# A decoder layer on one core: the last softmax sums on GpSimd, the gates spread by unit 14, two experts ahead of the shared one

## The chip, the cores and the metric

The kernel runs on one core of one Trainium2 chip. The metric is the time of one execution in microseconds on the device; the kernel before took 257.47 us (median of 3 runs, 257.4 to 257.64). TensorE, VectorE, ScalarE, GpSimd and the SyncE queue each run their own list of instructions in program order and meet only at semaphores.

## What is computed

One decoder layer over 2 batches of 256 tokens of width 256, normed after each block: self-attention with latent projections, cross-attention to 512 context rows with latent keys, and a mixture of 8 experts (2 picked per token) with one shared expert. The last stage is the one that matters here:

```python
def _moe(x, gate, expert_bias, w1, w2, w3, shared_w1, shared_w2, shared_w3):
    scores = sigmoid(xt @ gate.T)
    _, sel = top_k(scores + expert_bias, 2)
    ...
    for e in range(NUM_EXPERTS):
        h = silu(xb @ w1e.T) * (xb @ w3e.T)     # xb: the tokens times their gate
        out_r += where(expert_ids == e, h @ w2e.T, 0)
    out = (silu(xt @ shared_w1.T) * (xt @ shared_w3.T)) @ shared_w2.T
    return out + out_r
x = layernorm(x + self_attention(x))
x = layernorm(x + cross_attention(x, ctx_512))
x = layernorm(x + moe(x))
```

## The kernel before

Everything stays in on-chip memory. Cross-attention runs as 16 units (`NUNIT`), one per batch and pair of heads; units 0 to 7 are batch 0, units 8 to 15 batch 1. For a unit, `xmax` finds row maxima, `xexp` makes four 128x512 blocks of scores that ScalarE exponentiates into `probs`, GpSimd adds the four blocks of `probs` up into `psums` (L451, L455), TensorE takes the weighted sums of the four blocks (`xpv`, L858) and the product that turns `psums` into the softmax's denominators (`xsum`, L845), and VectorE takes the reciprocal (`xrecip`, L1443) and norms (`xnorm`, L1448, into `ctxn`). `out_proj(t, p)` (L872) multiplies unit p's `ctxn` with the output weights, for token tile t; tiles 0 and 1 are batch 0, tiles 2 and 3 batch 1. TensorE's loop over n works on `xmax` of unit n and `xexp` of unit n - 2, and closes with `xpv` and `xsum` of unit n - 3. So at its last two rounds, n = 16 and 17, TensorE has no maxima left and takes in the first steps of batch 0's experts.

The experts are 18 jobs (`JOBS`, 8 experts and the shared one for each batch; -1 is the shared one). Job q is `up(q)` on TensorE (L937), `silu(q)` on ScalarE (L1220), `hidden(q)` on VectorE (L1542) and `down(q)` on TensorE (L947, L950), which accumulates in the batch's bank on top of `base_rows` (L915, the residual). An expert's product is bf16, the shared expert's f32. An expert's input `xe` is the normed tokens `x2T` times the gate of the expert, spread over all partitions by `spread_gates(b, v)` on TensorE (L910, two experts at a time, into bank 7 or 6 for batch 0) and multiplied by `scaled(b, e)` on VectorE (L1484), for batch 1 half of it on GpSimd (L475). `spread_gates(0, v)` with v of 2 or 3 waits until the inputs of the pair that used its bank are scaled. The gates come from `gate_scores` (L882), a tanh (L1202), `routing` (nine small VectorE instructions, L1459 to L1478) and `gates_T` (L889, L1209).

Each norm is `norm_stats` on VectorE (L1349, L1351), `reciprocal_root` on GpSimd (L399, L401), `norm_apply` on VectorE (L1356); the norm after cross-attention also needs `normed_T` (L656, copied by L1148) to make `x2T`. The last norm ends in `y`, which SP stores tile by tile (L332).

All orders are written out by hand, one list for each engine. Around the change, before it:

- GpSimd adds up units 0 to 14; unit 15 is added up by VectorE (L1532, three adds with semaphore `xlast_sb`).
- TensorE: in round n = 16 `spread_gates(0, 0)`, in round 17 `(0, 1)` and `(0, 2)`, each round closed by `xpv` and `xsum`; `spread_gates(0, 3)` between unit 14's and unit 15's sums; then out_proj 6, up(0) (shared), a base row, out_proj 7, up(1), up(2) and so on (L1022 to L1062). up(2) waits until all eight inputs of batch 0 are scaled.
- VectorE: inputs 0 and 1 in round 16, 2 and 3 in round 17, then the three adds, the reciprocals of units 14 and 15, inputs 4 and 5, hidden(0), two sets of statistics, inputs 6 and 7, hidden(1) (L1490 to L1553).
- The last norm's tiles 0 and 1 (batch 0, whose last down is job 9) have both statistics behind hidden(13) and both `norm_apply` behind hidden(15); tiles 2 and 3 follow at the end.

Of the kernel before, what the change touches and what calls it, by code (L numbers as in the profile page):

```python
# [63 lines left out]
JOBS = ([(0, -1)] + [(0, e) for e in range(4)] + [(1, -1)] + [(0, e) for e in range(4, NE)]  # L64
# [4 lines left out]
def decoder_layer(nc, xT_in, pk_in, rope_in, spread_in, wE_in, wcT_in, wq_in, bv_up, xn_in, bo, wop_in, wu_in, sh_in,  # L69
                  kv_in, w13_in, w2_in, out):  # L70
    stack = ExitStack()
    with stack:
# [202 lines left out]
        xlast_sb = sem("xlast_sb")  # L275
# [61 lines left out]
        def _(pool):  # L337
# [105 lines left out]
            for n in range(NUNIT + LAG - 1):  # L443
# [42 lines left out]
        def up_bank(q):  # L486
            return 4 + q % 3
# [15 lines left out]
        def _(pe):  # L503
# [334 lines left out]
            def xsum(n):  # L838

                if n == NUNIT - 1:  # L840
                    pe.wait_ge(xlast_sb, NKC - 1)
                else:
                    pe.wait_ge(xadd_sb, 3 * n + 3)
# [74 lines left out]
            def up(q):  # L918
                b, e = JOBS[q]
                if q < 2:  # L920
                    pe.wait_ge(ctxn_sb, NUNIT - 1 + q)
                if q == 1:
                    pe.wait_ge(ld_moe, 32)
                if q == 2:
                    pe.wait_ge(xe_dve, NE)
# [30 lines left out]
            for n in range(NUNIT + LAG):  # L956
                for r in range(4):
# [50 lines left out]
                    if n == NUNIT + 1 and r == 3:  # L1008
                        out_proj(2, 5)
                        out_proj(3, 5)  # L1010
                        spread_gates(0, 2)
                    if n == 1 and r == 1:
# [9 lines left out]
            spread_gates(0, 3)  # L1022
# [5 lines left out]
            up(0)  # L1028
            pe.wait_ge(xexp_sb, NKC * NUNIT)
            base_rows(0, 0)  # L1030
            out_proj(2, 7)
            out_proj(3, 7)
            up(1)
            up(2)
            base_rows(0, 1)
            up(3)
            down(0)
            normed_T(1, x2, 2, 0)
            normed_T(1, x2, 3, 1)
            down(1)  # L1040
            up(4)
            gate_scores(1, bank(0))
            up(5)
            down(2)
            up(6)
            down(3)
            down(4)
            up(7)
            gates_T(1, bank(0))
            base_rows(1, 0)  # L1050
            spread_gates(1, 0)
            base_rows(1, 1)
            spread_gates(1, 1)
# [12 lines left out]
        def _(act):  # L1066
# [189 lines left out]
            for q in range(4):  # L1256
                silu(q)
            normed_T(1, x2T, 2, 0)
            normed_T(1, x2T, 3, 1)
            silu(4)  # L1260
            gate_exp(1, ps[:, 0, :])
            silu(5)
            silu(6)
            gates_T(1, ps[:, 0, :])
            silu(7)
            gates_out(1)
# [7 lines left out]
        def _(dve):  # L1274
# [215 lines left out]
            for n in range(NUNIT + LAG + 2):  # L1490
# [29 lines left out]
                if NUNIT <= n < NUNIT + 2:  # L1520
                    scaled(0, 2 * (n - NUNIT))
                    scaled(0, 2 * (n - NUNIT) + 1)
                if n == NUNIT + 1:

                    for kc in range(1, NKC):
                        dve.wait_ge(xexp_sb, NKC * (NUNIT - 1) + kc + 1)
                        if kc == 1:
# [148 lines left out]
```

## Time and profile before

| | before |
|---|---|
| median of 3 runs | 257.47 us (257.4 to 257.64) |
| profiled execution, time | 257.63 us |
| profiled execution, span | 255.9 us |
| busy: PE, DVE, ACT, POOL | 239.8, 196.0, 120.5, 115.9 us |

PE is TensorE's matmuls, DVE VectorE, ACT ScalarE, POOL GpSimd. In the rows below a number in brackets at the end of a line is the engine's idle time before it and what ended it. Matmuls are pipelined: a group's length in the timeline includes filling the pipeline and overlaps the next group; the chain of waits counts each group from the end of the one before, so its lengths add up. An f32 matmul stands as two records, so "x4" is two matmuls.

### The profile page before, as it was taken

The page shows a single profiled execution, that of the slowest core. Times are in us where ns is not written, and L with a number is a line of the kernel's source. Part 1 is how long each engine was busy: PE and PEld are TensorE (multiplying, and loading weights), DVE is VectorE, ACT ScalarE, POOL GpSimd, SP SyncE. Part 2 cuts the span into 40 slices and gives each one's busy share as a digit, 9 for nine tenths or more (in the row PEclk, how much of TensorE's full clock was granted, in tenths as well). Part 3 has the DMA queues.
Part 4 walks back from the last instruction along what each step waited for, and adds up shares of the span by engine and source line. Part 5 has one row for each costly group of instructions (what it writes and reads, how often), then busy time and mean ns, then how long its engine had stood idle before and what let it go on. Part 6 is the DMA issues. An engine that isn't in the chain of part 4 may idle for free.

```text
span 255.9 us, 4411 instructions
## 1 busy us (share of the span) xinstructions
PE 239.8 (94%) x1581; PEld 172.9 (68%) x1581; DVE 196.0 (77%) x351; ACT 120.5 (47%) x253; POOL 115.9 (45%) x167
## 2 busy tenths in 40 slices
PE   8989999988999999998999999999999999988991
PEld 5478797754656567775676767677776777767870
DVE  1377577899865999769889999986668895886684
ACT  2555367556366355454355655434325534313450
POOL 7297400000027437856487666666375534011272
PEclk9999999999999999999999999999999999999999
DMA  6999940000000840000000000000000000000002
GB/s 241 322 289 328 412 178 3 1 1 3 0 3 1 154 95 0 0 0 0 4 0 0 4 0 0 4 0 0 3 0 0 4 0 0 3 0 0 0 3 82
DMA packets 4500, 13.66 MB, mean 53 GB/s; under 512 B 512, under 2 KB 1280, under 8 KB 4352
## 3 DMA queue, kind: packets, MB, share of 16 engines
q1 hardware_dynamic: 4048, 11.29, 13.2%
q0 software_dynamic: 432, 2.10, 3.8%
q8 instruction: 13, 0.21, 0.4%
q14 instruction: 7, 0.06, 0.1%
HBM read 14.43 MB, written 0.52 MB: 58 GB/s over the span
## 4 chain that ended last, share of the span: by engine, by line
PE 76%; DVE 18%; ACT 3%; issue 2%; POOL 0%; POOLq 0%
PE ps L858 11%; PE ps L808 6%; PE ps L835 5%; PE ps L836 5%; PE ps L809 5%; PE ps L872 5%; PE ps L792 4%; DVE rcp L1334 3%; PE ps L509 3%; PE ps L648 3%; PE ps L937 3%; DVE mneg L1363 3%; PE ps L845 3%; PE ps L695 2%; DVE xmneg L1425 2%
## 5 line engine op out<-in xcount | busy, mean ns | idle before, releaser
L1198 ACT ACTIVATE probs<-ps 128x512 f32<-128x512 f32 x64 | 38.0, 597 | 57.0 <-PE ps L836 55.9
L1425 DVE TENSOR_REDUCE xmneg<-ps 128x1 f32<-128x512 f32 x64 | 43.2, 689 | 17.9 <-PE ps L809 17.5
L455 POOL TENSOR_TENSOR psums<-psums,probs 128x512 f32<-128x512 f32 x30 | 38.7, 1289 | 10.8 <-ACT probs L1198 8.2
L451 POOL TENSOR_TENSOR psums<-probs 128x512 f32<-128x512 f32 x15 | 19.2, 1283 | 31.1 <-ACT probs L1198 19.6
L808 PE MATMUL ps<-KA,QA 128*128 128x512 f32 x64 | 30.1, 470 | 2.1 <-DVE xmneg L1425 2.1
L858 PE MATMUL ps<-probs,kv_dup 128*64 128x256 f32 x256 | 31.2, 385 | 0.0
L1443 DVE RECIPROCAL xrcp<-ps 128x256 f32<-128x256 f32 x16 | 28.0, 1752 | 2.4 <-PE ps L845 2.4
L399 POOL TENSOR_TENSOR rstd<-mv,eps_col 128x1 f32<-128x1 f32 x12 | 2.3, 188 | 59.3 <-DVE mv L1351 59.0
L1363 DVE TENSOR_REDUCE mneg<-ps 128x4 f32<-128x1024 f32 x16 | 19.6, 1224 | 9.3 <-PE ps L588 8.9
L835 PE MATMUL ps<-QA,KA 128*128 128x512 f32 x64 | 26.0, 406 | 0.0
L836 PE MATMUL ps<-QB,KB 68*128 68x512 f32 x64 | 25.4, 397 | 0.0
L809 PE MATMUL ps<-KB,QB 68*128 68x512 f32 x64 | 25.2, 394 | 0.0
L858 PEld LDWEIGHTS ps<-probs,kv_dup 128*64 128x64 f32 x256 | 17.0, 136 | 11.2 <-ACT probs L1198 3.0
L1103 ACT ACTIVATE probs<-ps 128x512 f32<-128x512 f32 x32 | 17.3, 593 | 10.6 <-PE ps L614 10.5
L808 PEld LDWEIGHTS ps<-KA,QA 128*128 128x128 f32 x64 | 12.0, 188 | 11.9 <-DVE xmneg L1425 5.9
L792 PE MATMUL ps<-x1T,M_sb 128*128 128x256 f32 x64 | 16.4, 380 | 0.5 <-ACT x1T L1148 0.5
L872 PE MATMUL ps<-U_sb,ctxn 128*128 128x256 f32 x64 | 16.5, 380 | 0.0
L1190 ACT ACTIVATE QA<-ps 64x256 fp32r<-64x256 f32 x32 | 12.1, 378 | 8.8 <-PE ps L792 8.4
L1418 DVE TENSOR_TENSOR QB<-ps,QA 64x256 fp32r<-64x256 f32 x32 | 13.3, 416 | 3.7 <-ACT QA L1190 3.2
L1226 ACT ACTIVATE QB<-ps,own_rows 4x256 fp32r<-4x256 f32 x32 | 13.1, 455 | 4.9 <-PE ps L819 4.6
L1220 ACT ACTIVATE sil<-ps 128x256 f32<-128x256 f32 x18 | 6.9, 382 | 16.5 <-PE ps L937 15.5
L835 PEld LDWEIGHTS ps<-QA,KA 128*128 128x128 f32 x64 | 12.1, 190 | 3.3 <-issue 0.8
(165 smaller groups left out, 475.1 us busy)
## 6 DMA issues: line engine op xcount, KB each, us to landing
wu<-in_wu SPq DMA_DIRECT2D x4, 640.0 KB, 8.2
wq<-in_wq SPq DMA_DIRECT2D x4, 512.0 KB, 13.1
wcT<-in_wcT SPq DMA_DIRECT2D x4, 384.0 KB, 12.1
wE<-in_wE SPq DMA_DIRECT2D x4, 320.0 KB, 11.2
w13T<-in_w POOLq DMA_DIRECT2D x1, 1024.0 KB, 7.6
x1T<-in_xT SPq DMA_DIRECT2D x1, 512.0 KB, 3.7
kvp<-in_kv POOLq DMA_DIRECT2D x1, 512.0 KB, 6.1
x_nat<-in_xn SPq DMA_DIRECT2D x1, 512.0 KB, 18.0
```

The source lines that it names most:

```text
L455: g.tensor_tensor(psums[:, s, :], psums[:, s, :], probs[:, s, kc, :], ALU.add).then_inc(xadd_sb, 1)
L792: mm = pe.matmul(ps[:, query_bank(n), 0:SEQ], M_sb[:, c, p, :], x1T[:, c, b * SEQ:(b + 1) * SEQ], start=(c == 0), stop=(c == 1))
L808: pe.matmul(o, QA[:, s, hh, q], KA[:, b * LK:(b + 1) * LK], start=True, stop=False)
L809: pe.matmul(o, QB[:, s, hh, q], KB[:, b * LK:(b + 1) * LK], start=False, stop=True).then_inc(xmax_ps, 1)
L835: pe.matmul(o, KA[:, k0:k0 + P], QA[:, s, :, :], start=True, stop=False)
L836: pe.matmul(o, KB[:, k0:k0 + P], QB[:, s, :, :], start=False, stop=True).then_inc(xexp_ps, 1)
L858: mm = pe.matmul(ps[DC * hh:DC * hh + DC, 4 + n % 2, 0:SEQ], kv_dup[:, NKC * b + kc, 0, :], probs[:, n % 2, kc, hh * SEQ:(hh + 1) * SEQ], ...
L872: mm = pe.matmul(o, ctxn[:, p, t * P:(t + 1) * P], U_sb[:, p, :], start=(p == 0 and t < 2), stop=(p == NPAIR - 1))
L1198: a.activation(probs[:, n % 2, kc, :], ps[:, 2 + u % 2, :], ACT.Exp).then_inc(xexp_sb, 1)
L1363: v.tensor_reduce(mneg[:, i % 2, :, 2 * pr:2 * pr + 2].rearrange("p u h -> p h u"), ps[:, 0:2, :].rearrange("p h (u k) -> p h u k", u=2), ...
L1425: v.tensor_reduce(xmneg[:, n % 4, qt, hh:hh + 1], ps[:, u % 2, :], AX.X, ALU.max, negate=True).then_inc(xmax_sb, 1)
L1443: v.reciprocal(xrcp[:, n % 2, :], ps[:, 4 + n % 2, SEQ:2 * SEQ]).then_inc(xrcp_sb, 1)
```

## The change

GpSimd's loop takes one round more and adds up unit 15 too; VectorE's three adds and their semaphore go. `spread_gates(0, 3)` moves into round 17, behind `(0, 2)`; VectorE scales inputs 2 to 7 in a row in that round, ahead of the reciprocals of units 14 and 15. The first jobs become experts 0 and 1 and then the shared expert, with banks 4, 6, 5; up(0) and up(1) now stand ahead of out_proj 7, both base rows ahead of up(0), and it is up(1) that waits for all eight inputs. up(3), the transposes, gate scores, gates and base rows of batch 1 are put in another order on TensorE, ScalarE and VectorE; routing of batch 1 comes ahead of hidden(4). Of the last norm, tile 0's statistics stay behind hidden(13), tile 1's go behind hidden(15), and both `norm_apply` go behind the last hidden.

```diff
--- before.py
+++ after.py
@@ -61,7 +61,7 @@
 SH = 792
 LAG = 2
 NQ = 2 * LAG + 1
-JOBS = ([(0, -1)] + [(0, e) for e in range(4)] + [(1, -1)] + [(0, e) for e in range(4, NE)]
+JOBS = ([(0, 0), (0, 1), (0, -1), (0, 2), (0, 3), (1, -1)] + [(0, e) for e in range(4, NE)]
         + [(1, e) for e in range(NE)])
 LAST0 = 9
 
@@ -272,7 +272,6 @@
         xexp_ps = sem("xexp_ps")
         xexp_sb = sem("xexp_sb")
         xadd_sb = sem("xadd_sb")
-        xlast_sb = sem("xlast_sb")
         xsum_done = sem("xsum_done")
         xpv_done = sem("xpv_done")
         xrcp_sb = sem("xrcp_sb")
@@ -440,7 +439,7 @@
             g.affine_select(out=before[:], in_=before[:], pattern=[[1, NE], [-1, NE]], compare_op=ALU.is_gt, fill=0.0,
                             base=0, channel_multiplier=0).then_inc(const2, 1)
 
-            for n in range(NUNIT + LAG - 1):
+            for n in range(NUNIT + LAG):
 
                 m = n - LAG
                 if m >= 0:
@@ -484,7 +483,7 @@
 
 
         def up_bank(q):
-            return 4 + q % 3
+            return (4, 6, 5)[q % 3]
 
         def gates_bank(b, v):
             return (7, 6)[v % 2] if b == 0 else (7, 1)[v % 2]
@@ -837,10 +836,7 @@
 
             def xsum(n):
 
-                if n == NUNIT - 1:
-                    pe.wait_ge(xlast_sb, NKC - 1)
-                else:
-                    pe.wait_ge(xadd_sb, 3 * n + 3)
+                pe.wait_ge(xadd_sb, 3 * n + 3)
                 for hh in range(2):
                     mm = pe.matmul(ps[DC * hh:DC * hh + DC, 4 + n % 2, SEQ:2 * SEQ], ones64[:],
                                    psums[:, n % 2, hh * SEQ:(hh + 1) * SEQ], start=True, stop=True)
@@ -917,12 +913,13 @@
 
             def up(q):
                 b, e = JOBS[q]
-                if q < 2:
-                    pe.wait_ge(ctxn_sb, NUNIT - 1 + q)
+                if q == 0:
+                    pe.wait_ge(ctxn_sb, NUNIT - 1)
+                    pe.wait_ge(ld_moe, 32)
                 if q == 1:
-                    pe.wait_ge(ld_moe, 32)
+                    pe.wait_ge(xe_dve, NE)
                 if q == 2:
-                    pe.wait_ge(xe_dve, NE)
+                    pe.wait_ge(ctxn_sb, NUNIT)
                 if q >= 3:
                     pe.wait_ge(hid_sb, q - 2)
                 if e >= 0:
@@ -1009,6 +1006,7 @@
                         out_proj(2, 5)
                         out_proj(3, 5)
                         spread_gates(0, 2)
+                        spread_gates(0, 3)
                     if n == 1 and r == 1:
                         keep_warm(6)
                     if r == 1 and 1 <= n <= NUNIT:
@@ -1019,38 +1017,37 @@
                     for kc in range(NKC):
                         xpv(n - LAG - 1, kc)
                     xsum(n - LAG - 1)
-            spread_gates(0, 3)
             for kc in range(NKC):
                 xpv(NUNIT - 1, kc)
             xsum(NUNIT - 1)
             out_proj(2, 6)
             out_proj(3, 6)
-            up(0)
             pe.wait_ge(xexp_sb, NKC * NUNIT)
             base_rows(0, 0)
+            base_rows(0, 1)
+            up(0)
+            up(1)
             out_proj(2, 7)
             out_proj(3, 7)
-            up(1)
             up(2)
-            base_rows(0, 1)
-            up(3)
             down(0)
             normed_T(1, x2, 2, 0)
+            down(1)
             normed_T(1, x2, 3, 1)
-            down(1)
+            up(3)
             up(4)
             gate_scores(1, bank(0))
+            down(2)
             up(5)
-            down(2)
+            down(3)
+            gates_T(1, bank(0))
+            base_rows(1, 0)
+            base_rows(1, 1)
+            spread_gates(1, 0)
+            spread_gates(1, 1)
             up(6)
-            down(3)
             down(4)
             up(7)
-            gates_T(1, bank(0))
-            base_rows(1, 0)
-            spread_gates(1, 0)
-            base_rows(1, 1)
-            spread_gates(1, 1)
             down(5)
             for q in range(8, len(JOBS)):
                 up(q)
@@ -1253,17 +1250,18 @@
                         gate_exp(0, ps[:, 7, 0:SEQ])
                     if n == NUNIT and r == 2:
                         gates_T(0, ps[:, 7, 0:SEQ])
-            for q in range(4):
+            for q in range(3):
                 silu(q)
             normed_T(1, x2T, 2, 0)
             normed_T(1, x2T, 3, 1)
+            silu(3)
             silu(4)
             gate_exp(1, ps[:, 0, :])
             silu(5)
+            gates_T(1, ps[:, 0, :])
+            gates_out(1)
             silu(6)
-            gates_T(1, ps[:, 0, :])
             silu(7)
-            gates_out(1)
             for q in range(8, len(JOBS)):
                 silu(q)
                 if q == 9:
@@ -1517,21 +1515,12 @@
                     xnorm(n - LAG - 2)
                 if n + 2 < NUNIT:
                     query_lo(n + 2)
-                if NUNIT <= n < NUNIT + 2:
-                    scaled(0, 2 * (n - NUNIT))
-                    scaled(0, 2 * (n - NUNIT) + 1)
+                if n == NUNIT:
+                    scaled(0, 0)
+                    scaled(0, 1)
                 if n == NUNIT + 1:
-
-                    for kc in range(1, NKC):
-                        dve.wait_ge(xexp_sb, NKC * (NUNIT - 1) + kc + 1)
-                        if kc == 1:
-                            dve.wait_ge(xsum_done, NUNIT - 2)
-                        else:
-                            dve.wait_ge(xlast_sb, kc - 1)
-                        s = (NUNIT - 1) % 2
-                        v.tensor_tensor(psums[:, s, :], probs[:, s, 0, :] if kc == 1 else psums[:, s, :], probs[:, s, kc, :],
-                                        ALU.add).then_inc(xlast_sb, 1)
-
+                    for e in range(2, NE):
+                        scaled(0, e)
             def hidden(q):
 
                 dve.wait_ge(sil_sb, q + 1)
@@ -1541,36 +1530,31 @@
                     dve.wait_ge(down_done, q - 2)
                 v.tensor_tensor(dst, sil[:, q % 3, :], ps[:, up_bank(q), SEQ:2 * SEQ], ALU.mult).then_inc(hid_sb, 1)
 
-            scaled(0, 4)
-            scaled(0, 5)
             hidden(0)
             for t in (2, 3):
                 norm_stats(1, t, ps[:, t - 2, 0:D], None)
-            scaled(0, 6)
-            scaled(0, 7)
             hidden(1)
             for t in (2, 3):
                 norm_apply(1, t, x2, ps[:, t - 2, 0:D])
             hidden(2)
             hidden(3)
+            routing(1)
             hidden(4)
-            routing(1)
             hidden(5)
+            scaled(1, 0)
             hidden(6)
-            scaled(1, 0)
+            scaled(1, 1)
             hidden(7)
-            scaled(1, 1)
             for q in range(8, len(JOBS)):
                 hidden(q)
                 if q == 9:
                     scaled(1, 4)
                     scaled(1, 5)
-                if q == 13:
-                    for t in range(2):
-                        norm_stats(2, t, ps[:, 2, t * D:(t + 1) * D], None)
-                if q == 15:
-                    for t in range(2):
-                        norm_apply(2, t, y, ps[:, 2, t * D:(t + 1) * D])
+                if q in (13, 15):
+                    t = q // 15
+                    norm_stats(2, t, ps[:, 2, t * D:(t + 1) * D], None)
+            for t in range(2):
+                norm_apply(2, t, y, ps[:, 2, t * D:(t + 1) * D])
             for t in (2, 3):
                 norm_stats(2, t, ps[:, 3, (t - 2) * D:(t - 1) * D], None)
             for t in (2, 3):
```

## Rows read from the trace of the kernel before

**Rows 1.** The page: busy time, share of the span and instructions of each engine.

```profile
PE 239.8 (94%) x1581; PEld 172.9 (68%) x1581; DVE 196.0 (77%) x351; ACT 120.5 (47%) x253; POOL 115.9 (45%) x167
```

**Rows 2.** The chain of waits, 219.5 to 240 us: start, length (us), engine, target, line.

```profile
219.73 0.23 PE ps L910 x2
219.97 1.88 PE ps L858 x16
221.85 0.43 PE ps L845 x4
222.28 0.43 PE ps L910 x2
...
225.06 1.77 DVE xrcp L1443
...
231.74 0.43 PE ps L915 x2
232.17 0.44 PE ps L937 x4
...
234.56 0.99 PE ps L882 x8
235.56 1.83 PE ps L937 x8
...
239.60 0.50 PE ps L910 x2
```

**Rows 3.** TensorE's timeline: start, length (us), line, operation, idle before and releaser.

```profile
224.95 1.13 PE L872 MATMUL ps<-U_sb,ctxn 128*128 128x256 f32 x4
...
231.12 0.61 PE L937 MATMUL ps<-xe,w13T 128*128 128x256 bf16 x4 [1.59 <-DVE xe L1484]
...
248.34 0.39 PE L950 MATMUL ps<-w2T,hid 128*128 128x256 bf16 x2 [0.37 <-DVE hid L1542]
...
250.08 0.72 PE L950 MATMUL ps<-w2T,hid 128*128 128x256 bf16 x4 [0.69 <-DVE hid L1542]
```

**Rows 4.** VectorE's timeline, same columns.

```profile
217.97 1.29 DVE L1484 TENSOR_TENSOR xe<-x2T,ps 128x512 bf16<-128x512 f32 x2
...
219.97 1.49 DVE L1532 TENSOR_TENSOR psums<-psums,probs 128x512 f32<-128x512 f32 x2
...
228.72 0.43 DVE L1349 BATCH_NORM_STATS2 stats<-ps 128x6 f32<-128x256 f32 x1
...
231.31 0.99 DVE L1356 TENSOR_SCALAR x<-ps,mv,rstd 128x256 f32<-128x256 f32 x2
...
235.81 0.17 DVE L1459 TENSOR_SCALAR gsc<-gexp 128x16 f32<-128x16 f32 x1 [0.38 <-ACT gexp L1202]
...
237.83 0.17 DVE L1478 TENSOR_TENSOR ghl<-gsc,ghl 128x16 fp32r<-128x16 f32 x1
...
248.54 1.16 DVE L1356 TENSOR_SCALAR y<-ps,mv,rstd 128x256 f32<-128x256 f32 x2
249.61 0.74 DVE L1542 TENSOR_TENSOR hid<-sil,ps 128x256 bf16<-128x256 f32 x2
```

**Rows 5.** By line: durations min/median/max (ns) of L1484, L1432; the stores' landing (us).

```profile
L1484 DVE TENSOR_TENSOR xe<-x2T,ps x12: 655/680/687, 213.4 to 244.1; 128x512 bf16<-128x512 f32 x12
...
L1432 DVE CAST xmhi<-xmneg x16: 170/780/1132, 86.4 to 203.5; 128x4 fp32r<-128x4 f32 x16
...
DMA to landing us min/median/max: 1.7/1.7/1.7
```

**Rows 6.** GpSimd's timeline, same columns as Rows 3.

```profile
211.83 2.69 POOL L455 TENSOR_TENSOR psums<-psums,probs 128x512 f32<-128x512 f32 x2 [0.66 <-ACT probs L1198]
...
230.50 0.55 POOL L401 TENSOR_TENSOR rstd<-rstd,mhalf 128x1 f32<-128x1 f32 x1
```

**Rows 7.** ScalarE's timeline, same columns as Rows 3.

```profile
218.43 1.08 ACT L1198 ACTIVATE probs<-ps 128x512 f32<-128x512 f32 x2 [0.93 <-PE ps L836]
...
227.84 0.38 ACT L1220 ACTIVATE sil<-ps 128x256 f32<-128x256 f32 x1 [7.03 <-PE ps L937]
```

## The prediction

> **What bounds the kernel now.** I read the page first: TensorE is busy for 94% of the span [rows 1], so the span is TensorE's work plus its gaps, and an edit that only reorders work can gain no more than gaps. Then I read the chain of waits from 219.73 us, where TensorE is done with out_proj 5. There the reader is to see unit costs, each from end to end: a gate spread 0.23, the four weighted sums of a unit 1.88, its softmax-sum product 0.43, and 0.20 more for whatever comes behind such a product (the spread behind it 0.43 instead of 0.23) [rows 2]. Third, TensorE's own timeline with its idle times [rows 3]. After 219 us it has four gaps that the change could touch:
> - the up-projection up(2) waits 1.59 us for VectorE's last scaled inputs, and pays 0.17 to refill (0.61 for a group of 0.44 [rows 2, 3]): 1.76;
> - the first gate spread of batch 1 waits for its gate rows, 0.50 for a group of 0.23 [rows 2]: 0.27;
> - down(14) waits 0.37 behind VectorE, with the refill 0.54 [rows 3];
> - down(16) and down(17) wait 0.69 and take 0.72 for 0.44 of work [rows 3]: 0.97.
>
> Together 3.54 us. TensorE's work is the same before and after (same matmuls in another order), so the forecast is: the gaps that remain, and what the end of the kernel then costs.
>
> **The last sums to GpSimd.** VectorE loses three additions, 0.7 us each [rows 4]; GpSimd gets three at 1.35 (2.69 for two [rows 6]). The last exponential of unit 15 ends at 219.51 [rows 7]. Even if all three adds waited for that, they would end at 219.51 + 4.04 = 223.55; taken as the exponentials come, near 221.8. TensorE gets to the product that needs them at 224.58 (below), so they cost nothing; the cover is at least 0.8 and likely 2.5 us. GpSimd's next instruction, a norm's root, is wanted after 228 us.
>
> The rows say 1.35 against 0.7, and that the slower place has room. The Trainium skill, page "GPSIMD Engine Reference", section "4.1 Engine selection", speaks against this edit: elementwise adds of two inputs belong on VectorE, GpSimd being about twice as slow. On the ratio the trace agrees (1.9). Charged as if on the path, the edit would cost 3 x 0.65 = 1.9 us and the sum below would come to 257.2; I don't take that, since the path is TensorE's.
>
> **All spreads by unit 14, six inputs in a row.** The fourth spread now stands ahead of unit 14's weighted sums. It waits for inputs 2 and 3, which end at 217.97 + 1.29 = 219.26 [rows 4], before TensorE is there. TensorE's ends: spreads 219.96 and 220.19, weighted sums 222.07, product 222.50, then 1.88 + 0.20 gives 224.58, and 225.03 for the last product. Before it was the same 225.03: one spread merely changed places.
>
> VectorE is the tight part. It idles from 219.26 until the third spread is out (220.00), scales four inputs (0.68 each, starts 0.61 apart: 1.29 for a pair [rows 4, 5]) until 222.51, and only then takes unit 14's reciprocal, whose input is there at 222.54. 1.77 for that [rows 2], 0.42 for the product that norms it (hidden's shape, of which two take 0.74 with overlap [rows 4]) and two hops of 0.04 bring unit 14 to 224.77. A group of TensorE that waited runs 0.22 after its release (a hop and the refill): out_proj 6 could start at 224.99, against TensorE's 225.03. So cost nothing, slack 0.04; past that, VectorE's lateness is paid one for one. Unit 15's reciprocal then starts when its product is ready, at 225.06 as before [rows 2], and unit 15 ends at 227.29 as before.
>
> The unknown here is four scalings beside GpSimd's adds. From below: zero. The nearest rows are the twelve scalings of the trace, 655 to 687 ns, the first of them at 213.4 [rows 5], beside the adds of 211.83 to 214.52 [rows 6]: four times 0.007 is 0.03. I take zero; the upper end is rival 4.
>
> **Two experts ahead of the shared one.** From out_proj 6's end at 226.08 [rows 3]: two base rows of 0.43 give 226.95, up(0) and up(1) of 0.44 give 227.83 [rows 2]. All eight inputs are there since 222.5, so the 1.76 gap is gone. out_proj 7 (0.86) ends at 228.69, its first half at 228.26. up(2), now the shared expert (1.83 [rows 2]), ends at 230.52; down(0), the transpose of tile 2 and down(1), 0.22 each, 231.18. What is late next is batch 1's norm. Before, its first statistics started at 228.72 [rows 4] and the second root ended at 231.05 [rows 6]: 2.33. Now the statistics start at 228.30, so the root ends at 230.63; applying it takes 0.55 (0.99 and 1.16 for two [rows 4]) and the refill 0.22, so the second transpose can run at 231.4 to 231.5. **New gap 0.3.**
>
> From 231.7: up(3), up(4), and the gate scores (0.99 [rows 2]) end at 233.6. Before, the routing started 0.26 after the scores' end (235.55) and took until 238.00, 2.19 [rows 2, 4]; now that is 236.05, usable by TensorE at 236.27. It has down(2) (0.86), up(5) (1.83) and down(3) (0.22) to do until 236.5. No gap, slack 0.2; hidden(4) stands behind the routing on VectorE, and is wanted only at 238.4. Both base rows (0.86) then cover the copy of the gate rows, so the 0.27 gap goes too. On ScalarE, silu(6) and silu(7) now queue behind the copy of the gates: 0.1 us, under down(5)'s 0.86. GpSimd's four scalings start almost 3 us earlier.
>
> **The last norm.** In the loop over batch 1's experts TensorE takes 0.66 each; a hidden ends 0.88 after its up-projection (activation 0.38 [rows 7], product 0.42, two hops). One set of statistics (0.6) behind hidden(13) instead of two leaves down(14) a gap of 0.02 for 0.54. The other set stands between hidden(15), which ends at 246.48, and hidden(16), which then ends at 247.38, usable at 247.60, where TensorE is free at 247.16: 0.44. hidden(17) follows by 0.44, one product more than down(16) covers: 0.22. TensorE ends at 248.3. But both norm_apply (1.16 with a wait [rows 4], 1.0 without) now stand in front of the last statistics, which start at 248.66 where TensorE's end would have allowed 248.30: **0.36 lost**. The stores of the first two tiles follow the norm_apply, at 248.3 and 248.8, and the third tile's at 250.8; each lands in 1.7 us [rows 5], so they are out of the way.
>
> **Sum.** Gaps 3.54 before, 0.30 + 0.02 + 0.44 + 0.22 = 0.98 after: 2.56 gained; 0.36 given back at the end: 2.2 net. The profiled execution's 257.63 us (span 255.9) becomes 255.4 (span 253.7). The median of the three runs is 0.16 below the profiled one: 257.47 - 2.2 = **255.3 us**.
>
> **Rivals.**
> 1. The norm of batch 1 gets no shorter without the scalings that stood in it. Before, from its first statistics (228.72) to both tiles normed (231.31 + 0.99 = 232.30 [rows 4]) it took 3.58; then the second transpose runs at 228.30 + 3.58 + 0.22 = 232.1, a gap of 0.9 for 0.3: 255.9. Against: two scalings, 1.3 us of VectorE, have left that stretch.
> 2. The end keeps its old gaps, since statistics still stand between the last hiddens: 1.51 for 0.68, +0.83: 256.1. For it: VectorE's work there is only shifted. Against: per expert of 0.66 it has 0.24 spare.
> 3. Both, or a VectorE late by 1.2 to 1.6 us at out_proj 6: 256.7, which would be near no change.
> 4. Slower: GpSimd's adds and VectorE's scalings shut each other out, instruction by instruction. Then six scalings (4.08) and two to three adds stand in one row from 217.97: 224.74 to 226.09 for 222.51. Unit 14 is 2.2 to 3.6 late, and with it out_proj 6 and all behind it. Middle 2.9: 258.2. It turns slower by a measurable amount from 2.7 us of lateness. For it: VectorE's four-column cast takes anything from 0.17 to 1.13 us [rows 5], so something does hold that engine up at times. Against: none of the twelve scalings was held up. The Trainium skill, page "SBUF — State Buffer", section "Who interferes with whom", has such a lock, for VectorE instructions in a two-port mode or with two SBUF inputs; it spares those with one SBUF input, as the scalings are (their other input is in PSUM). By that rule this rival is out, and the 655 to 687 ns agree.
> 5. The change does not do what it says, because GpSimd's sums come too late: only from 2.3 us per add on, against 1.35.
>
> **How the numbers follow.** Forecast 0.73; rival 1 0.10; rival 2 0.09; rival 3 0.04; rivals 4 and 5 0.04 together (5 taken at the same 258). Around the forecast itself I allow 0.4 to 0.5: slacks of 0.04 and 0.2 are worked out closer than hops are known. Below, 254.8: the 0.36 at the end and the 0.20 behind a softmax-sum product could partly go. Above, past rivals 1 and 2: 256.3. Outside are rivals 3 to 5 and the tails, under 0.2. A measurement of this kernel tells 0.2% (0.5 us) from no change. Faster by more (under 256.95): 0.92; within: 0.04; slower: 0.04.
>
> **What would show it.** GpSimd's three adds end near 221.8; the six scalings run from 218.0 to 219.3 and from 220.0 to 222.5, 0.65 to 0.69 each; out_proj 6 starts at 225.0 as now. No idle before an up-projection near 231, but 0.1 to 0.5 before a transpose. Batch 1's first spread at 237.5 instead of 239.6. TensorE's last matmul ends near 248.3, and the last statistics start 0.4 later, behind two norm_apply. A start of out_proj 6 past 225.3, an idle over 0.8 at the transpose, or idle time in front of unit 14's weighted sums would prove me wrong.

## The result, and the profile after

The changed kernel takes 255.34 us (median of six, 254.99 to 256.25), the kernel before 257.75 in the runs beside it (257.4 to 258.8). The ratio is 0.9901, with a 95% interval of 0.9882 to 0.9921. The profiled execution took 255.44 us, with a span of 253.7 instead of 255.9.

Some executions here (among them the profiles of e3, e10 and e12) have a stretch near 57 to 61 us, before anything that the change touches, in which TensorE runs at its lower clock, and their way from there to out_proj 5 is 0.5 to 0.8 us longer. So I compare kernels by the *tail*: from the start of out_proj 5 on TensorE to the start of the last `norm_apply` on VectorE. Before, that is 218.71 to 253.21: 34.50 us. After, it is 218.93 to 250.97: 32.04. The lines that mark it, two of before and the first of after (the other one of after closes VectorE's timeline below):

```profile
218.71 1.03 PE L872 MATMUL ps<-U_sb,ctxn 128*128 128x256 f32 x4
253.21 0.54 DVE L1356 TENSOR_SCALAR y<-ps,mv,rstd 128x256 f32<-128x256 f32 x1 [0.24 <-POOL rstd L401]
218.93 1.03 PE L868 MATMUL ps<-U_sb,ctxn 128*128 128x256 f32 x4
```

The change is worth **2.46 us** there; the forecast was 2.2. The tail starts 0.22 later in the profile of after, which is why the span shows 2.2. Times of after stand 0.22 later than the forecast's for that reason alone.

The page of the kernel after, busy time of each engine, which answers to [rows 1]:

```profile
PE 238.6 (94%) x1581; PEld 172.7 (68%) x1581; DVE 194.2 (77%) x348; ACT 120.6 (48%) x253; POOL 119.8 (47%) x170
```

TensorE has the same number of matmuls in a span that is 2.2 us shorter; VectorE has three instructions less, GpSimd three more and 3.9 us more work, at no cost. TensorE's timeline of after (start, length, line, operation, rows * columns of the weights, idle before and its releaser), to be read beside [rows 3]:

```profile
222.13 0.60 PE L841 MATMUL ps<-psums,ones 128*64 128x256 f32 x4
222.56 1.90 PE L854 MATMUL ps<-probs,kv_dup 128*64 128x256 f32 x16
224.29 0.60 PE L841 MATMUL ps<-psums,ones 128*64 128x256 f32 x4
225.05 1.13 PE L868 MATMUL ps<-U_sb,ctxn 128*128 128x256 f32 x4 [0.16 <-DVE ctxn L1446]
...
226.88 1.04 PE L934 MATMUL ps<-xe,w13T 128*128 128x256 bf16 x8
...
230.85 0.38 PE L947 MATMUL ps<-w2T,hid 128*128 128x256 bf16 x2
231.36 0.44 PE L655 MATMUL ps<-ident,x 128*128 128x128 f32 x2
231.63 1.04 PE L934 MATMUL ps<-xe,w13T 128*128 128x256 bf16 x8
232.50 0.96 PE L878 MATMUL ps<-sh,x2T 128*128 128x8 f32 x8
...
237.10 0.82 PE L906 MATMUL ps<-gate_rows,pick 128*128 128x256 f32 x4
...
246.76 0.38 PE L947 MATMUL ps<-w2T,hid 128*128 128x256 bf16 x2
247.40 0.84 PE L947 MATMUL ps<-w2T,hid 128*128 128x256 bf16 x4 [0.26 <-DVE hid L1531]
```

Up(0) and up(1) run at 226.88 in one piece, where an up-projection used to wait 1.59. The new gap is at the second transpose: a group of two takes 0.22 on the path, so it could have come at 231.07; it starts at 231.36 and takes 0.06 more, together 0.35. Batch 1's spreads start at 237.10 with no gap. At the end the last two downs start 0.42 late and take 0.24 more than 0.60: 0.66 in place of 0.54 + 0.97.

VectorE's timeline of after, same columns, beside [rows 4]:

```profile
218.19 1.29 DVE L1482 TENSOR_TENSOR xe<-x2T,ps 128x512 bf16<-128x512 f32 x2
220.23 2.48 DVE L1482 TENSOR_TENSOR xe<-x2T,ps 128x512 bf16<-128x512 f32 x4 [0.75 <-PE ps L906]
222.78 1.76 DVE L1441 RECIPROCAL xrcp<-ps 128x256 f32<-128x256 f32 x1
224.57 0.42 DVE L1446 TENSOR_TENSOR ctxn<-ps,xrcp 128x256 f32<-128x256 f32 x1
...
246.94 0.85 DVE L1531 TENSOR_TENSOR hid<-sil,ps 128x256 bf16<-128x256 f32 x2
247.71 0.99 DVE L1354 TENSOR_SCALAR y<-ps,mv,rstd 128x256 f32<-128x256 f32 x2
248.62 0.42 DVE L1347 BATCH_NORM_STATS2 stats<-ps 128x6 f32<-128x256 f32 x1
...
250.97 0.55 DVE L1354 TENSOR_SCALAR y<-ps,mv,rstd 128x256 f32<-128x256 f32 x1 [0.24 <-POOL rstd L400]
```

Unit 14 is normed at 224.99, just after TensorE is free at 224.89: that is the 0.16 idle ahead of out_proj 6. At the end both `norm_apply` stand between the last hidden and the last statistics, 248.62, 0.38 behind TensorE's last matmul (248.24).

GpSimd's timeline of after, beside [rows 6]:

```profile
217.79 1.29 POOL L450 TENSOR_TENSOR psums<-probs 128x512 f32<-128x512 f32 x1 [3.06 <-ACT probs L1195]
219.32 2.69 POOL L454 TENSOR_TENSOR psums<-psums,probs 128x512 f32<-128x512 f32 x2 [0.24 <-ACT probs L1195]
```

The sums are ready at 222.01; TensorE asks for them at 224.29. VectorE's four scalings run beside the adds at 0.60 apart, with no sign of a lock: 2.48 for the four, and 2.47 in e4, where no add runs beside them.

### The profile page after: what moved, and what is told of

Read it like the earlier page. It is cut to its first block, busy times and chain, and to the rows that moved or that the text cites. A ratio compares the mean times of both kernels' runs of the same rounds, so it can differ in the third digit from the quotient of the medians.

```text
span 253.7 us, 4411 instructions
## 1 busy us (share of the span) xinstructions
PE 238.6 (94%) x1581; PEld 172.7 (68%) x1581; DVE 194.2 (77%) x348; ACT 120.6 (48%) x253; POOL 119.8 (47%) x170
## 4 chain that ended last, share of the span: by engine, by line
PE 70%; DVE 16%; DMA 5%; issue 2%; ACT 2%; SPq 2%; POOL 1%; POOLq 0%
PE ps L854 10%; PE ps L807 6%; PE ps L868 5%; PE ps L834 5%; PE ps L835 5%; PE ps L808 5%; DMA wq<-in_wq 5%; PE ps L791 5%; DVE rcp L1332 3%; PE ps L934 3%; PE ps L647 3%; DVE mneg L1361 3%; PE ps L841 2%; DVE xmneg L1423 2%; PE ps L709 2%
## 5 line engine op out<-in xcount | busy, mean ns | idle before, releaser
L454 POOL TENSOR_TENSOR psums<-psums,probs 128x512 f32<-128x512 f32 x32 | 41.2, 1287 | 11.2 <-ACT probs L1195 8.5
L450 POOL TENSOR_TENSOR psums<-probs 128x512 f32<-128x512 f32 x16 | 20.5, 1281 | 34.2 <-ACT probs L1195 22.6
L1332 DVE RECIPROCAL rcp<-sums 128x256 f32<-128x256 f32 x8 | 14.0, 1748 | 0.3 <-ACT sums L1107 0.2
```

The lines of the kernel that those rows point to most:

```text
L454: g.tensor_tensor(psums[:, s, :], psums[:, s, :], probs[:, s, kc, :], ALU.add).then_inc(xadd_sb, 1)
```

## The experiments

"After" is the changed kernel. Theory: the gain is TensorE's idle time taken away, most of it the 1.59 before up(2), and GpSimd's sums are what makes the early inputs possible. Rivals: the gain comes from VectorE's three adds alone; from the order of the jobs; or two engines hinder each other, so that the early scalings would cost as much as they bring.

| kernel | median us | ratio to before, 95% | tail us |
|---|---|---|---|
| before | 257.75 | | 34.50 |
| after | 255.34 | 0.9901 (0.9882 to 0.9921) | 32.04 |
| e8, after again | 255.62 | 0.9917 (0.9892 to 0.9942) | 32.05 |
| e2, before + sums on GpSimd | 257.85 | 1.0003 (0.9975 to 1.0032) | 34.50 |
| e10, e2 + early inputs | 256.07 | 0.992 (0.9897 to 0.9944) | 32.62 |
| e12, e10 + new last norm | 255.73 | 0.9872 (0.9835 to 0.9909) | 32.12 |
| e1, after, sums on VectorE | 258.95 | 1.0017 (0.999 to 1.0044) | 35.77 |
| e11, e1 + wait filled | 257.18 | 0.9958 (0.9941 to 0.9975) | 34.07 |
| e4, after, late inputs | 259.19 | 1.0031 (1.0007 to 1.0054) | 35.77 |
| e7, after + three adds | 256.89 | 0.9963 (0.9937 to 0.9988) | 33.58 |
| e5, after, shared expert first | 256.59 | 0.995 (0.9923 to 0.9977) | 33.10 |
| e3, after, old last norm | 256.89 | 0.9933 (0.9905 to 0.996) | 32.56 |
| e6, after, base rows first | 255.02 | 0.9903 (0.9865 to 0.994) | 31.82 |
| e9, four fills | 254.66 | 0.9872 (0.9845 to 0.9899) | 31.38 |

Ratios are to runs of before on the same chip, whose medians differ (257.71 beside e5, e6, e8 and e9, 258.79 beside e12), so small differences are read from the tails.

**e8: the changed kernel again**, as the yardstick among the others.

> The changed kernel once more, beside the kernels of this group: 255.3 us, the reference for the others here.

255.62 us, tail 32.05 against 32.04: tails repeat to 0.01.

**e2: the sums alone.** The kernel before with unit 15's adds on GpSimd; nothing else.

```diff
-            for n in range(NUNIT + LAG - 1):
+            for n in range(NUNIT + LAG):
...
-                if n == NUNIT - 1:
-                    pe.wait_ge(xlast_sb, NKC - 1)
-                else:
-                    pe.wait_ge(xadd_sb, 3 * n + 3)
+                pe.wait_ge(xadd_sb, 3 * n + 3)
...
-                    for kc in range(1, NKC):
-                        ...
```

> The kernel before (257.5 us) with only one part of the change: GpSimd adds up unit 15. Theory: the 1.76 us gap in front of up(2) stays, since inputs 4 to 7 still stand behind both reciprocals, so within 0.2 of before: 257.3 to 257.6. Rival (freeing VectorE of 2.1 us of adds is the gain by itself): 255.3 to 255.6.

257.85 us, a tail of exactly 34.50. TensorE's timeline of e2 has the old wait, of the old length:

```profile
231.06 0.61 PE L933 MATMUL ps<-xe,w13T 128*128 128x256 bf16 x4 [1.59 <-DVE xe L1480]
```

The adds stood in a place where VectorE had to wait anyway. Taking 2 us of work from it there, by itself, is worth nothing.

**e1: the rest without the sums.** After, with the three adds back on VectorE behind its six scalings (GpSimd's loop and `xsum`'s wait go back with them).

```diff
...
                     for e in range(2, NE):
                         scaled(0, e)
+                    for kc in range(1, NKC):
+                        ...
+                        v.tensor_tensor(psums[:, s, :], probs[:, s, 0, :] if kc == 1 else psums[:, s, :],
+                                        probs[:, s, kc, :], ALU.add).then_inc(xlast_sb, 1)
```

> The changed kernel (255.3 us), but VectorE adds up unit 15 again, behind its six scalings. Theory (TensorE's gaps set the time; VectorE's row up to unit 14's reciprocal is tight): three adds of 0.7 us take VectorE from 222.7 to 224.85, unit 14's reciprocal starts 2.07 later, TensorE waits as much longer in front of out_proj 6, and nothing behind it gets the time back: 257.4. Rival (adds are better placed on the engine that does them in half the time): the sums are there no later, and the time is 255.3 or less.

The tail became 35.77: 3.73 longer than after's, where 2.07 was expected, and 1.3 longer than before's. TensorE's timeline of e1, the groups that follow the late norm of unit 14:

```profile
224.86 0.65 PE L845 MATMUL ps<-psums,ones 128*64 128x256 f32 x4 [0.50 <-DVE psums L1536]
226.99 1.50 PE L872 MATMUL ps<-U_sb,ctxn 128*128 128x256 f32 x4 [1.48 <-DVE ctxn L1450]
228.28 1.91 PE L915 MATMUL ps<-x,ident 128*128 128x256 f32 x4
229.99 1.55 PE L938 MATMUL ps<-xe,w13T 128*128 128x256 bf16 x8
```

The waits, 0.50 and 1.48, are about what the adds should bring. But the two base rows then take 1.91 (1.03 for the same group in after) and eight up-projection matmuls 1.55 (1.04 at 226.88 in after). The table of stretches of e1 (start:end, length, then busy time of PE, PEld, DVE, ACT, POOL with counts, granted clock, DMA share, GB/s):

```profile
219.50:226.90 7.40, 5.51 (x46) 3.29 (x44) 6.53 (x10) 1.42 (x2) 0.00 (x0) 1.00 0.01 2
226.90:230.40 3.50, 3.41 (x10) 2.50 (x11) 2.12 (x3) 0.00 (x0) 0.00 (x0) 0.60 0.00 0
```

The granted clock is 0.60 in the 3.5 us behind the waits: TensorE fell to its lower level (1.2 GHz instead of 2.4) for most of it. That was not in the expectation. So the excess needed a test of its own.

**e11: e1 with the wait filled.** Fourteen small matmuls, whose results are cleared later, stand in front of out_proj 6; everything else is e1.

```diff
             xsum(NUNIT - 1)
+            pe.wait_ge(xexp_sb, NKC * NUNIT)
+            ones = ident[:].bitcast(BF16)
+            for _ in range(14):
+                pe.matmul(ps[:, 3, 0:2 * P], ones[:, 0:P], ones, start=True, stop=True)
             out_proj(2, 6)
```

> The kernel with unit 15's adds back on VectorE, and 14 dummy matmuls of 0.11 us in TensorE's wait in front of out_proj 6. The kernel without them was 3.6 us of span slower than the changed one where I expected 2.1, and its matmuls ran at half rate behind a wait of 1.48. Theory (the 1.5 us too much are a spell of TensorE at its lower clock that the wait brings): with the wait filled the matmuls behind it run at full rate and the span is 1.4 to 1.5 shorter, 257.4. Rival (the half rate has another cause than the wait): no shorter, 258.9.

257.18 us, tail 34.07: 1.70 shorter than e1 with more work in it. TensorE's timeline of e11, and under it the same stretch of the table:

```profile
225.24 1.70 PE L1030 MATMUL ps<-ident 128*128 128x256 bf16 x14
226.78 1.13 PE L872 MATMUL ps<-U_sb,ctxn 128*128 128x256 f32 x4
227.75 1.03 PE L915 MATMUL ps<-x,ident 128*128 128x256 f32 x4
```

```profile
226.90:230.40 3.50, 3.50 (x22) 3.02 (x22) 2.62 (x4) 0.77 (x2) 0.00 (x0) 1.00 0.00 0
```

The clock is full and the groups have their usual lengths. What is left against after is 2.03, the 2.07 expected for three adds on the path. So in the company of the early inputs the move to GpSimd is worth 2.03 us, and 3.73 with the clock in the profiled execution, though alone it is worth nothing. The lower clock does not come every time: three of e1's twelve executions take 256.95 to 257.71, near e11's 257.18, at a granted clock of 0.995 to 0.996 on the mean of the execution; the other nine take 258.21 to 260.05 at 0.982 to 0.990.

**e4: the inputs late again.** After, with the fourth spread behind unit 14's product and inputs 4 to 7 scaled behind unit 15's norm.

```diff
                         spread_gates(0, 2)
-                        spread_gates(0, 3)
...
-                    for e in range(2, NE):
-                        scaled(0, e)
+                    scaled(0, 2)
+                    scaled(0, 3)
...
+            for e in range(4, NE):
+                scaled(0, e)
             hidden(0)
```

> The changed kernel, but the fourth spread stands between the sums of units 14 and 15 again and inputs 4 to 7 are scaled behind unit 15's norm. Theory: VectorE scales from 227.15 to 229.6, up(1) runs at 229.8 instead of 227.3, out_proj 7 and the norm of batch 1 stand behind it: a gap of 2.3 to 2.5 us, 257.6 to 257.8, nothing left of the gain. Rival (the new order of the jobs is the gain, since it puts base rows and up(0) ahead of the wait): at least half of the gain stays, 256.5 or less.

Tail 35.77, 3.73 longer than after's; 2.3 to 2.5 had been expected. TensorE's timeline of e4:

```profile
229.61 1.04 PE L934 MATMUL ps<-xe,w13T 128*128 128x256 bf16 x4 [2.35 <-DVE xe L1482]
230.44 1.91 PE L868 MATMUL ps<-U_sb,ctxn 128*128 128x256 f32 x4
```

The wait, 2.35, is what was expected, and slow groups follow it as in e1: out_proj 7 takes 1.91 instead of 1.03. The granted clock from 229.6 to 233.0 is 0.54. The wait alone takes 2.35 of the gain of 2.46; the other 1.38 of the 3.73 goes with the slow groups, which no run separates here as e11 does for e1. So an early up-projection gains nothing unless its inputs are early too, and with the lower clock it is a loss.

**e10: sums and early inputs alone.** The kernel before with GpSimd's sums (the lines of e2), four spreads by unit 14 and six inputs in a row; jobs, gates, transposes and last norm as before.

```diff
...
                         spread_gates(0, 2)
+                        spread_gates(0, 3)
...
+                if n == NUNIT + 1:
+                    for e in range(2, NE):
+                        scaled(0, e)
...
-            scaled(0, 4)
-            scaled(0, 5)
             hidden(0)
-            scaled(0, 6)
-            scaled(0, 7)
             hidden(1)
```

> The kernel before (257.5) with two parts of the change, the sums on GpSimd and the early fourth spread with six inputs scaled in a row; the old order of jobs, gates and norms stays. Theory from the gaps: up(2)'s 1.76 goes and 0.3 in front of unit 15's weighted sums; the old order keeps its gap at the gates and those at the end: 255.6. Rival (the new order of the jobs is needed to use the inputs, as the kernel with the shared expert first in the new order lost 1.1 us): 256.5.

Tail 32.62: 1.88 of the 2.46, where 1.9 was expected. TensorE's timeline of e10, in the old order of jobs:

```profile
229.82 1.04 PE L933 MATMUL ps<-xe,w13T 128*128 128x256 bf16 x8
...
232.43 0.60 PE L655 MATMUL ps<-ident,x 128*128 128x128 f32 x4
...
238.71 0.50 PE L906 MATMUL ps<-gate_rows,pick 128*128 128x256 f32 x2
```

Up(1) and up(2) run through, and both transposes too: the old order has no new gap there. What is left of the old gaps is the late gate spread (0.50 for two), a wait at the gate scores and the two waits at the end (0.37 and 0.69, as in [rows 3]).

**e12: e10 with the new last norm**, so that after differs from it by the order of jobs, gates and transposes alone.

```diff
-                if q == 13:
-                    for t in range(2):
-                        norm_stats(2, t, ps[:, 2, t * D:(t + 1) * D], None)
-                if q == 15:
-                    for t in range(2):
-                        norm_apply(2, t, y, ps[:, 2, t * D:(t + 1) * D])
+                if q in (13, 15):
+                    t = q // 15
+                    norm_stats(2, t, ps[:, 2, t * D:(t + 1) * D], None)
+            for t in range(2):
+                norm_apply(2, t, y, ps[:, 2, t * D:(t + 1) * D])
```

> The kernel before with the sums on GpSimd, the six early inputs and the last norm as changed; only the order of jobs, gates and transposes stays old. From out_proj 5's start to the last norm_apply the kernel before takes 34.50 us, the changed one 32.04, the kernel with the early inputs alone 32.62, and putting the old norm back into the changed kernel cost 0.52. Theory (the inputs and the norm are the gain, the order of the jobs adds next to nothing): 32.62 - 0.52 = 32.10, the time of the changed kernel, 255.3 to 255.4. Rival (the norm's place only pays with the new order of jobs): 32.4 or more, 255.7 or more.

Tail 32.12, where 32.10 was expected. The norm's new place is worth 0.50 here, and the whole reordering of the jobs, gates and transposes 0.08. That is a balance, not an order without effect: in the chains of waits the reordering takes 0.27 from the first gate spread of batch 1 (0.50 for 0.23 in e12) and 0.21 from the gate scores (1.00 in e12, 0.79 in after), and brings the 0.35 at the transpose.

**e3: the old last norm.** After, with the lines of e12's diff turned round.

> The changed kernel with the last norm of tiles 0 and 1 where it was: both statistics behind hidden(13), both applied behind hidden(15). Theory: down(14) gets its 0.54 gap back (0.52 more), down(16) and down(17) 0.97 for 0.66 (0.31 more), and the last statistics follow TensorE's end at once (0.34 less): 255.8. Rival (the statistics' place costs nothing because the last hiddens wait for ScalarE anyway): the 0.34 alone counts, 255.0.

Tail 32.56, 0.52 longer than after's; 0.49 was expected. TensorE's timeline of e3 has the two waits of [rows 3] back:

```profile
247.55 0.39 PE L947 MATMUL ps<-w2T,hid 128*128 128x256 bf16 x2 [0.38 <-DVE hid L1531]
...
249.28 0.72 PE L947 MATMUL ps<-w2T,hid 128*128 128x256 bf16 x4 [0.69 <-DVE hid L1531]
```

**e5: the shared expert first.** After, with one line of the job list.

```diff
-JOBS = ([(0, 0), (0, 1), (0, -1), (0, 2), (0, 3), (1, -1)] + ...
+JOBS = ([(0, -1), (0, 0), (0, 1), (0, 2), (0, 3), (1, -1)] + ...
```

> The changed kernel with the jobs of batch 0 in the old order (the shared expert ahead of experts 0 and 1), all else as changed. Theory (the order matters because out_proj 7, and with it the norm of batch 1, must not stand behind the 1.73 us of the shared up-projection, and because that is the cover for the norm): the norm starts 1.3 later, gaps of 0.65 and 0.34 at the transposes for 0.35, and 0.5 at the gates of batch 1: about 1.1 more, 256.4. Rival (only the scaled inputs mattered; they are there in time in either order): 255.3 to 255.5.

Tail 33.10: 1.06 longer (1.1 expected). TensorE's timeline of e5:

```profile
232.17 0.44 PE L655 MATMUL ps<-ident,x 128*128 128x128 f32 x2 [0.48 <-DVE x L1354]
...
237.57 0.39 PE L885 MATMUL ps<-ident,ghl 128*16 128x128 f32 x2 [0.32 <-DVE ghl L1476]
```

With the shared up-projection (1.73) ahead, out_proj 7 and with it the norm and the routing come later, while the new order has less work left to cover them. Each order needs its own arrangement behind it: inside the new one the two experts must be first, yet against the whole old order they bring 0.08.

**e7: how much cover GpSimd has.** After, with three more adds ahead of unit 15's, which are overwritten.

```diff
+                    if m == NUNIT - 1:
+                        for k in range(3):
+                            g.tensor_tensor(psums[:, s, :], probs[:, s, 0, :], probs[:, s, 1, :], ALU.add).then_inc(slow, 1)
+                            pool.wait_ge(slow, k + 1)
```

> The changed kernel with three more adds of 1.3 us on GpSimd ahead of unit 15's (the first add, repeated). In the changed kernel's trace the sums end at 222.0 and the product that needs them starts at 224.3, so theory (2.2 us of cover, beyond it one for one): the sums end 3.9 later, at 225.9, the product 1.7 later, out_proj 6 1.4 later: 256.7, and 258.2 if a gap of that length is followed by a spell of TensorE at its lower clock, as the ones of 2.0 and 2.4 us in the two kernels with VectorE late were. Rival (the adds on GpSimd are on the path already): 3.9 later at least, 259.2.

Tail 33.58, 1.54 longer: the variant of the expectation in which the clock stays full. TensorE's timeline of e7:

```profile
225.92 0.65 PE L846 MATMUL ps<-psums,ones 128*64 128x256 f32 x4 [1.55 <-POOL psums L459]
```

and GpSimd's:

```profile
223.19 2.67 POOL L459 TENSOR_TENSOR psums<-psums,probs 128x512 f32<-128x512 f32 x2
```

The sums end at 225.86, counted from the tail's start 3.94 later than in after, and the cover there is 2.28 (222.01 to 224.29). So the product starts 1.72 later, counted likewise, and out_proj 6, which in after waits for VectorE anyway, 1.54. The adds cost nothing only as long as there is cover, and beyond it they count in full.

**e6: base rows ahead of out_proj 6**, to fill the 0.16 wait for unit 14's norm.

```diff
+            pe.wait_ge(xexp_sb, NKC * NUNIT)
+            base_rows(0, 0)
+            base_rows(0, 1)
             out_proj(2, 6)
             out_proj(3, 6)
-            pe.wait_ge(xexp_sb, NKC * NUNIT)
-            base_rows(0, 0)
-            base_rows(0, 1)
```

> The changed kernel with batch 0's two base rows ahead of out_proj 6 instead of behind it. Theory (after the change it is VectorE's norm of unit 14 that out_proj 6 waits for, TensorE being there 0.3 us earlier): the base rows fill that wait, no idle is left in front of out_proj 6 and up(0) runs 0.23 earlier: 255.1. Rival (out_proj 6 still follows TensorE's own last product, as I predicted): 255.3, nothing moves.

Tail 31.82: 0.22 gained (0.23 expected). TensorE's timeline of e6:

```profile
224.00 0.60 PE L841 MATMUL ps<-psums,ones 128*64 128x256 f32 x4
224.53 1.13 PE L911 MATMUL ps<-x,ident 128*128 128x256 f32 x4
225.50 1.03 PE L868 MATMUL ps<-U_sb,ctxn 128*128 128x256 f32 x4
```

The base rows now stand behind the product, and out_proj 6 follows with no wait.

**e9: four fills.** e6, up(3) ahead of the second transpose, up(17) right behind up(16), and tile 1's `norm_apply` behind the last statistics.

```diff
-            normed_T(1, x2, 3, 1)
             up(3)
+            normed_T(1, x2, 3, 1)
...
             norm_apply(2, 0, y, ps[:, 2, 0:D])
+            for t in (2, 3):
+                norm_stats(2, t, ps[:, 3, (t - 2) * D:(t - 1) * D], None)
+            norm_apply(2, 1, y, ps[:, 2, D:2 * D])
```

> Four fills of gaps that the trace of the changed kernel shows: base rows ahead of out_proj 6 (0.23); up(3) between down(1) and the second transpose (0.15 of the 0.35 gap); up(17) right behind up(16), with down(14) to down(17) after it (0.22 of the 0.66 in front of the last downs); tile 1's norm_apply behind the statistics of tiles 2 and 3 instead of ahead of them (0.34). Theory (each gap is TensorE's or the end's own, so the gains add): 0.94 less, 254.4. Rival (VectorE's row is full, a gap that is filled opens at the next wait): 255.0 to 255.3.

254.66 us, tail 31.38: 0.66 shorter than after's and the shortest of all; 0.94 was expected. TensorE's timeline of e9, then VectorE's:

```profile
231.31 0.38 PE L655 MATMUL ps<-ident,x 128*128 128x128 f32 x2
231.53 0.60 PE L934 MATMUL ps<-xe,w13T 128*128 128x256 bf16 x4
232.26 1.03 PE L878 MATMUL ps<-sh,x2T 128*128 128x8 f32 x8
...
247.22 0.72 PE L947 MATMUL ps<-w2T,hid 128*128 128x256 bf16 x4 [0.26 <-DVE hid L1535]
```

```profile
247.41 0.54 DVE L1358 TENSOR_SCALAR y<-ps,mv,rstd 128x256 f32<-128x256 f32 x1
247.98 0.43 DVE L1351 BATCH_NORM_STATS2 stats<-ps 128x6 f32<-128x256 f32 x1
```

The transpose no longer waits, but the gate scores behind it do: they start at 232.26 where up(4) is done at 231.97. Filling that gap moved it one step on and was worth nothing. The statistics start 0.04 behind TensorE's last matmul (247.94), so the end's 0.33 came in full; base rows 0.22. That leaves 0.11 of the 0.22 expected of the early up(17): the last downs still wait 0.26, for hiddens that take their own time after the last up-projection. Beside after's second run on the same chip (255.62) the median is 0.96 lower; the tail, which repeats to 0.01, is the measure.

## Why the prediction was right

**The sum.** In tails, the forecast was 3.54 of gaps before, 0.98 after, 0.36 given back. Measured: 0.35 + 0.02 + 0.66 = 1.03 of gaps after, 0.34 given back (0.38 behind TensorE's end, where 0.04 is a hop). That is 2.17, and two things that the sum did not have bring it to 2.49, against 2.46 in tails. One is 0.20 at the gate scores: their 0.99 in [rows 2] I took for work, but 0.79 is what they take in the chain of waits of after, so part of it was a wait for the transposed copy. The other is 0.12 at out_proj 6. That the median came within 0.04 of the forecast is in part luck: the tail gained 0.26 more than the 2.2 of the sum, and the profiled execution of after reached its tail 0.22 later than that of before.

**The sums on GpSimd.** Forecast to end near 221.8: 222.01 with the 0.22 shift. The price of nothing held (e2), the cover of 2.5 was 2.28 (e7). What the prediction did not say is that this edit carries the others: without it they gain 0.43 at the full clock (e11's 34.07 against 34.50), and with the lower clock that comes with the wait they lose 1.27 (e1's 35.77). The Trainium skill's "GPSIMD Engine Reference", section "4.1 Engine selection", would leave adds to VectorE because GpSimd is slower. The ratio is as stated (1.29 against 0.69 in e1), but the conclusion goes the other way here: 2.03 us gained, since the slower engine had room and the faster one stood on the path.

**Six inputs in a row.** The scalings came out as worked out, and rival 4 (a lock between GpSimd and VectorE) is out: 2.48 for four beside the adds. The Trainium skill's "SBUF — State Buffer", section "Who interferes with whom", exempts instructions with one SBUF input, and these rows agree. Unit 14 was normed at 224.99, the forecast's 224.77 with the shift.

**The term that was mis-sized**: "0.20 more for whatever comes behind such a product". Behind unit 14's product unit 15's weighted sums start with no surcharge: 222.56 to 224.29 on their group is 1.73, not 1.88 + 0.20. In [rows 2] the spread behind the product loads 128 columns of weights after 64, and the sums behind a spread 64 after 128; after has 64 behind 64 there. So TensorE was ready 0.36 earlier than forecast, the slack of 0.04 turned negative, and VectorE's norm, not TensorE, sets out_proj 6. Only 0.12 of the 0.36 came through; e6 got 0.22 more of it.

**Two experts ahead of the shared one.** The 1.76 gap went, but I put it down to this part, and e10 shows it gone in the old order. What the reordering does by itself is 0.08 (e12). The forecast of the new gap at the transpose, 0.3, was right (0.35), and rival 1 (0.9) is out.

**The last norm.** TensorE's end was forecast at 248.3 and came at 248.24, 0.28 earlier once the 0.22 shift is taken off, from the two items above; the end's own terms, 0.44 + 0.22 and 0.36, were measured as 0.66 and 0.34, and e3 and e12 give 0.52 and 0.50 for the part. Rival 2 (1.51) is out. Rivals 3 and 5 are out with the others.

**Left open.** Which waits bring the lower clock: below. I did not separate the reordered gates from the reordered jobs in the 0.08.

## What to carry to other kernels

Cost a set of edits as a set: here one edit is worth 0.00 alone and 2.03 in company, another 0.08 that one would have credited with the whole 1.76, and only leaving out one part at a time, from both ends, tells. When TensorE is nearly gapless, look for the engine that becomes late next by a few hundredths, and for a group that is ready to run in that place. A gap that is filled may move to the next step of the same latency chain (norm, transpose, copy, gate scores), so follow that chain to its end before counting the gain.

## What the runs showed of the hardware

**A wait can cost twice.** In e1 the waits of 0.50 and 1.48 were followed by a stretch with a granted clock of 0.60, in e4 the wait of 2.35 by one of 0.54; e1's cost 1.70 (e1 against e11) on top of the wait itself. But the wait of 1.55 in e7 and that of 1.59 in [rows 3] were followed by none in the profiled executions: the table of stretches of e7 reads

```profile
225.90:229.40 3.50, 3.48 (x21) 2.72 (x22) 2.20 (x3) 0.38 (x1) 0.00 (x0) 1.00 0.00 0
```

The length of the wait alone does not decide, since 1.48 brought it and 1.59 did not; e1 had the other wait just ahead. Nor is it the same each time behind the same work: near 57 us, in a part that all these kernels share, TensorE waits 1.08 in the profile of before and 1.07 in that of e3. Before keeps a granted clock of 1.00 there, and e3's table of stretches reads

```profile
57.00:61.00 4.00, 4.00 (x22) 2.47 (x22) 3.25 (x6) 1.47 (x3) 0.00 (x0) 0.59 0.00 0
```

In e10 and e12 it is 0.65 and 0.64, behind 1.08 in both. So one profile without the lower clock, as of e7, does not show that the kernel never has it, and e1's times above point the same way. No run tells what decides.

**A surcharge between kinds of weights.** Where loads of 64 columns and of 128 follow each other, the group took 0.15 to 0.20 us more than its matmuls (1.88 against 1.73 for the same sixteen records; 0.43 against 0.23 for two spreads, [rows 2]); between groups of 64 columns nothing. Whether it is the number of columns or something else that changes with it, no run separates.
